# A three-layer decoder kernel: earlier neighbour similarities and their first load, first keys turned later, convolution in two bursts

## The reference

```python
na = jnp.maximum(jnp.sqrt(jnp.sum(a * a, axis=1)), EPS)
nb = jnp.maximum(jnp.sqrt(jnp.sum(b * b, axis=1)), EPS)
return jnp.sum(a * b, axis=1) / (na * nb)
```

## Time and profile before

| | |
|---|---|
| median of 3 runs | 1401.61 us (1400.67 to 1402.39) |
| profiled execution, its own time | 1403.73 us |
| its span, first to last instruction | 1401.7 us |
| PE busy | 1361.5 us (97%) |
| DVE busy | 1095.8 us (78%) |
| POOL busy | 978.7 us (70%) |
| ACT busy | 933.2 us (67%) |
| DMA queue of SP, share of 16 engines | 56.8% |

### The profile page before, as it was taken

One profiled execution on the slowest core, in us unless ns is written; L12 is line 12 of the kernel. 1 busy time (PEld: TensorE's weight loads), 2 busy tenths in 40 slices (PEclk: granted clock), 3 DMA queues, 4 the chain that ended last, 5 costly groups with the idle time before them and its releaser, 6 DMA issues.

```text
span 1401.7 us, 32338 instructions
## 1 busy us (share of the span) xinstructions
PE 1361.5 (97%) x8306; PEld 1058.0 (75%) x8306; DVE 1095.8 (78%) x3874; ACT 933.2 (67%) x3262; POOL 978.7 (70%) x932
## 2 busy tenths in 40 slices
PE   8999999999999999999997899999999999999996
PEld 5777777777777777777764688888888888888884
DVE  5887787778777777878785588777887788877877
ACT  5887888878788878878785455455554555545544
POOL 4777777767677776777775677667776677766762
PEclk9999999999999999999998999999999999999999
DMA  7344545455454545445468756676666766677652
GB/s 264 96 146 124 158 116 165 115 150 140 125 158 116 159 113 159 128 136 158 132 198 235 173 163 157 167 160 160 165 155 168 157 161 166 155 169 153 163 119 75
DMA packets 109005, 213.03 MB, mean 152 GB/s; under 512 B 26656, under 2 KB 32288, under 8 KB 108960
## 3 DMA queue, kind: packets, MB, share of 16 engines
q1 hardware_dynamic: 108624, 211.73, 56.8%
q10 hardware_dynamic: 336, 0.79, 0.2%
HBM read 131.83 MB, written 34.47 MB: 119 GB/s over the span
## 4 chain that ended last, share of the span: by engine, by line
PE 77%; SPq 6%; DMA 5%; issue 3%; DVE 3%; ACT 3%; POOL 2%; ACTq 0%; DVEq 0%; POOLq 0%
PE wo_ps L479 27%; PE wo_ps L1187 23%; PE conv_ps L1201 9%; SPq L320 4%; PE s_ps L509 4%; PE ffn_ps L1230 4%; PE pv_ps L522 3%; DMA raw<-in_xT 3%; PE ffn_ps L1249 3%; PE ffn_ps L1220 2%; ACT pexp L767 1%; PE turn_ps L498 1%; DVE sm L618 1%; DMA pt<-in_wqkv 1%; DMA att<-sim_scratch 1%
## 5 line engine op out<-in xcount | busy, mean ns | idle before, releaser
L479 PE MATMUL wo_ps<-weights,halves 128*128 128x512 f32 x2304 | 570.8, 399 | 2.8 <-DVE weights L681 2.8
L479 PEld LDWEIGHTS wo_ps<-weights,halves 128*128 128x128 f32 x2304 | 422.4, 189 | 137.7 <-issue 53.5
L767 ACT ACTIVATE pexp<-sm,smin 128x128 f32<-128x128 f32 x1024 | 398.0, 391 | 97.4 <-DVE smin L618 96.6
L1187 PE MATMUL wo_ps<-weights,halves 128*128 128x512 f32 x1464 | 395.1, 402 | 1.5 <-PEq L143 1.5
L1652 POOL TENSOR_TENSOR prods<-prod,prods 128x512 fp32r<-128x512 f32 x186 | 251.9, 1361 | 130.3 <-ACT prods L1513 125.2
L906 POOL TENSOR_TENSOR pn<-pexp,prec 128x512 f32<-128x512 f32 x256 | 265.4, 1041 | 96.2 <-DVE prec L625 96.1
L1187 PEld LDWEIGHTS wo_ps<-weights,halves 128*128 128x128 f32 x1464 | 268.1, 190 | 59.2 <-issue 2.4
L618 DVE CUSTOM_DVE_ANT_0 sm<-s_ps,mask_t 128x128 f32<-128x128 f32 x1024 | 232.0, 282 | 24.2 <-PE s_ps L509 21.8
L1513 ACT CAST prods<-prod 128x512 fp32r<-128x512 f32 x189 | 117.3, 621 | 167.0 <-DVE prod L1367 129.1
L767 ACT ACTIVATION_READ_ACCUMULATOR pexp<-sm,smin 128x1 f32 x1024 | 193.2, 189 | 0.0
L1367 DVE TENSOR_TENSOR prod<-att,x 128x512 f32<-128x512 f32 x189 | 183.0, 982 | 12.8 <-DMA att<-sim_scratch 10.1
(11 more groups left out here) (131 smaller groups left out, 1676.2 us busy)
## 6 DMA issues: line engine op xcount, KB each, us to landing
att<-sim_scratch SPq DMA_DIRECT2D x192, 252.0 KB
pt<-blocks SPq DMA_DIRECT2D x636, 64.0 KB, 2.0
ctx_t<-in_ctx SPq DMA_DIRECT2D x32, 576.0 KB, 5.2
raw<-in_xT SPq DMA_DIRECT2D x32, 512.0 KB, 4.0
xn<-in_x SPq DMA_DIRECT2D x32, 512.0 KB, 7.7
ot_scratch<-ot SPq DMA_DIRECT2D x63, 256.0 KB, 2.1
raw<-ot_scratch SPq DMA_DIRECT2D x31, 512.0 KB, 7.0
out<-late SPq DMA_DIRECT2D x31, 512.0 KB, 6.3
```

The source lines that it names most:

```text
L479: mm = pe.matmul(qkv_ps[(par + g) % 2][:], xs[:, par, xl, k], w_sb[:, wl, g, k], start=(k == 0 and n == 0), stop=(k == KT - 1 and n == 2))
L767: ins = nc.scalar.activation(pexp[:, c % 2, i * P:(i + 1) * P], sm[:, c % 2, i * P:(i + 1) * P], ACT.Exp, bias=smin[:, c % 2, i:i + 1], sc ...
L1187: mm = pe.matmul(wo_ps[n][:], os_t[:, par, ol, k], wo_sb[:, wl, k, n * BANK:(n + 1) * BANK], start=(k == 0 and m == 0), stop=(k == KT - 1 ...
```

## The change

- **Start.** PE turns the first keys ahead of slot 19 and no longer 16; POOL adds the first keys before it clears `pt`.
- **Similarities.** The sums are clamped by EPS squared before the root (in the step before the last, in place of a clamp of one column), and the clamp behind the root goes. `cosines` makes both products first and finishes `right` before `own`.
- **Stores.** ACT stores rows 0 and 1 behind its last moves of probabilities; SP stores rows 3 and 4, then row 2, and all this ahead of `store_first_half`.
- **First load.** `att` and its semaphores belong to both stages. At the end of stage one SP waits for all stores and starts the load of the first half for batch 0; stage two starts with the second half.
- **Bursts.** The six units of convolution stand ahead of slot 13 (three) and slot 4 of the next step (three), behind the expansion, which moves from slot 3 to 4. Both turns of x2 stand ahead of slot 12. The first batch keeps its own slots.
- **DVE** averages the first statistics behind `low_lt`. The buffer for dynamic DMA is set to 1024 bytes.

```diff
-    cs_edge = sem("cs_edge")
+    cs_bound = sem("cs_bound")
@@ sync, store_sims
             sp.wait_ge(sim_made, 1)
+            for n in (3, 4):
+                sp.dma_start(sim_row(sim_dram, n, 0), right).then_inc(sim_out, 16)
+            sp.wait_ge(sim_made, 2)
             sp.dma_start(sim_row(sim_dram, 2, 0), own).then_inc(own_out, 16)
-            sp.wait_ge(sim_made, 2)
-            for n, shift in ((0, 1), (1, 1), (3, 0), (4, 0)):
-                sp.dma_start(sim_row(sim_dram, n, shift), right).then_inc(sim_out, 16)
@@ sync, step of stage one
             if at_step(t, LAST):
+                store_sims()
                 store_first_half(b)
-                store_sims()
+                sp.wait_ge(own_out, 16)
+                sp.wait_ge(sim_out, 16 * 6)
+                start_att(sp, att, att_in, sim_dram, 0, 0)
@@ tensor, first batch
-                    if s == 2 * KT:
+                    if s == 2 * KT + 3:
                         pe.wait_ge(consts_in, 48)
                         turn_k(0, 0)
@@ vector
             dve.wait_ge(root, 1)
-            dve.tensor_scalar(norm, norm, COS_EPS, None, ALU.max).then_inc(cos_step, 1)
+            dve.reciprocal(norm, norm).then_inc(cos_step, 1)
+        def cosines():
             dve.wait_ge(cos_step, 1)
-            dve.reciprocal(norm, norm).then_inc(cos_step, 1)
+            dve.tensor_tensor(right, norm[:, 0:QD], norm[:, 1:QD + 1], ALU.mult).then_inc(cos_step, 1)
+            dve.tensor_tensor(own, norm[:, 0:QD], norm[:, 0:QD], ALU.mult).then_inc(cos_step, 1)
+            dve.wait_ge(cos_step, 2)
+            dve.tensor_tensor(right, right, nbs, ALU.mult).then_inc(sim_made, 1)
+            dve.wait_ge(cos_step, 3)
+            dve.tensor_tensor(own, own, sqs[:, 0:QD], ALU.mult).then_inc(sim_made, 1)
@@ vector, step B, p == 3
-                    edge = sqs[:, QD:QD + 1]
-                    dve.tensor_scalar(edge, edge, 0.0, None, ALU.max).then_inc(cs_edge, 1)
+                    dve.tensor_scalar(norm, sqs, COS_EPS * COS_EPS, None, ALU.max).then_inc(cs_bound, 1)
@@ scalar
+        def store_sims():
+            act.wait_ge(sim_made, 1)
+            for n in (0, 1):
+                act.dma_start(sim_row(sim_dram, n, 1), right).then_inc(sim_out, 16)
...
-            nc.scalar.activation(norm, sqs, ACT.Sqrt).then_inc(root, 1)
+            nc.scalar.activation(norm, norm, ACT.Sqrt).then_inc(root, 1)
...
                 if p == 7 and at_step(t, LAST):
+                    store_sims()
                     read_ot(b, 0)
@@ gpsimd
-        pool.wait_ge(w_lo, PIECES - STAGES + STAGES // 2)
-        pool.memset(pt[:], 0.0).then_inc(set_up, 1)
...
                 add_k(0, 0)
+                pool.wait_ge(w_lo, PIECES - STAGES + STAGES // 2)
+                pool.memset(pt[:], 0.0).then_inc(set_up, 1)
                 add_q(0, 0, 0)
@@ stage two
-    CONV_AT = (9, 11, 13, 15, 17, 20)
+    CONV_AT = (13, 13, 13, 20, 20, 20)
...
-        sp.wait_ge(sim_out, 16 * 6)
-        load_att(0, 0)
         load_att(0, 1)
@@ tensor, step of stage two
-                if valid(f) and s + SLOTS2 in conv_at(f):
-                    convolve(f, conv_at(f).index(s + SLOTS2))
-                if valid(c) and s in conv_at(c):
-                    convolve(c, conv_at(c).index(s))
                 if valid(z):
                     if s == 1:
                         turn_low(z)
-                    if s == 3:
+                    if s == 4:
                         expand(z)
+                for m in range(UNITS):
+                    if valid(f) and conv_at(f)[m] == s + SLOTS2:
+                        convolve(f, m)
+                    if valid(c) and conv_at(c)[m] == s:
+                        convolve(c, m)
                 if valid(f):
-                    if s in (11, 12):
-                        turn_x2(f, par, s - 11)
+                    if s == 12:
+                        turn_x2(f, par, 0)
+                        turn_x2(f, par, 1)
@@ tensor, behind the steps
+        convolve(B - 2, 3)
+        turn_low(B - 3)
         convolve(B - 2, 4)
-        turn_low(B - 3)
         convolve(B - 2, 5)
@@ vector, step of stage two
+            if valid(z):
+                low_lt(z)
+            if valid(c):
                 average(c, 0)
             if valid(z):
-                low_lt(z)
```

More of the change, by code:

```diff
@@ L124, in build @@
         kept = both.enter_context(nc.sbuf_tensor("kept", [P, D // 4 + BANK], F32))
+        att = both.enter_context(nc.sbuf_tensor("att", [P, TAPS, D], F32))
         handoff = (
@@ L139, in build @@
             both.enter_context(nc.sbuf_tensor("xn1", [P, D], F32)),
-            (kept[:, 0:D // 4], kept[:, D // 4:]))
+            (kept[:, 0:D // 4], kept[:, D // 4:]),
+            att, [both.enter_context(nc.semaphore(f"att_in{n}")) for n in range(2)])
         with ExitStack() as ctx:
@@ L165, in part1 @@
     (xn0, xn_in, o_in, o_hi, o_lo, wo_done, ot_out, ot_read, sim_made, sim_out,
-     added0, counted0, y0, stats0, xn1, kept) = handoff
+     added0, counted0, y0, stats0, xn1, kept, att, att_in) = handoff
     rope_t = sb("rope_t", [P, 2, 2, 1, DH])
@@ L728, in step @@
                 invert_norms()
-                cosine(0)
-                cosine(1)
+                cosines()
                 add_first(1)
@@ L969, in _, with start_att @@
         steps(pool, step, 0, LAST, LEAD, TAIL)
+def start_att(sp, att, att_in, sim_dram, t, h):
+    cols = slice(h * BANK, (h + 1) * BANK)
+    for (first, last), row in zip(RUNS, (0, 2, 3)):
+        sp.dma_start(att[first:last, :, cols],
+                     sim_dram[t, row, cols].unsqueeze(0).unsqueeze(0).broadcast_to([last - first, TAPS, BANK])
+                     ).then_inc(att_in[h], 16)
+    rows = sim_dram[t, 0:TAPS, cols]
+    both_edges = bass.AP(tensor=rows.tensor, offset=rows.offset, ap=[[2 * (D + SIM_PAD), 2]] + [list(d) for d in rows.ap])
+    sp.dma_start(att[EDGES[0]:EDGES[1] + 1:EDGES[1] - EDGES[0], :, cols], both_edges).then_inc(att_in[h], 16)
 def sim_row(sim_dram, n, shift):
@@ L1000, in part2 @@
     x1 = sb("x1", [P, 2, D + 2])
-    att = sb("att", [P, TAPS, D])
     prod = sb("prod", [P, PB, BANK])
@@ L1028, in part2 @@
     set_up = sem("set_up2")
-    att_in = [sem("att_in0"), sem("att_in1")]
     added = [added0] + [sem(f"added{n}") for n in range(1, 3)]
@@ L1129, in load_att @@
         def load_att(t, h):
-            cols = slice(h * BANK, (h + 1) * BANK)
             wait(sp, prod_done, after(t - 1, UNITS, TAPS * (h + 1)))
-            for (first, last), row in zip(RUNS, (0, 2, 3)):
-                sp.dma_start(att[first:last, :, cols],
-                             sim_dram[t, row, cols].unsqueeze(0).unsqueeze(0).broadcast_to([last - first, TAPS, BANK])
-                             ).then_inc(att_in[h], 16)
-            rows = sim_dram[t, 0:TAPS, cols]
-            both_edges = bass.AP(tensor=rows.tensor, offset=rows.offset, ap=[[2 * (D + SIM_PAD), 2]] + [list(d) for d in rows.ap])
-            sp.dma_start(att[EDGES[0]:EDGES[1] + 1:EDGES[1] - EDGES[0], :, cols], both_edges).then_inc(att_in[h], 16)
-        sp.wait_ge(sim_out, 16 * 6)
-        load_att(0, 0)
+            start_att(sp, att, att_in, sim_dram, t, h)
         load_att(0, 1)
```

5 lines of the change are left out of this document (2 added, 3 removed).

## The result

| | before | after |
|---|---|---|
| median (six runs each) | 1402.81 us | 1395.01 us (1392.16 to 1395.94) |
| ratio | | 0.9944 (95%: 0.9932 to 0.9957) |
| profiled execution, its own time | 1403.73 us | 1392.16 us |
| its span | 1401.7 us | 1390.1 us |

The change takes 7.8 us off the median; 7.1 were forecast, to 1394.5. On two other occasions, each beside the kernel before on one chip, the changed kernel's ratio was 0.9961 (0.9949 to 0.9973) and 0.9961 (0.9948 to 0.9973), which is 5.5 us. The three intervals overlap, so the gain is 5.5 to 7.8 us. The two profiled executions differ by 11.6 us; why that is too much is the first thing to see.

The account below looks back on a forecast made before the run. PE was taken as the bound nearly everywhere, except at the ends and handover, where it waits. Terms -1.9 - 3.0 - 1.7 - 0.5 = -7.1 us took the median from 1401.6 to 1394.5 us, range 1391.0 to 1399.0.

Parts of the forecast that it names:

- Start, -1.9: Stage one's start: PE no longer waits for the first keys, -1.9 us, between -1.0 and -2.1.
- Similarities and stores, -1.4 in the arrival: Handover: last store issued 1.9 us earlier, so att's first half reaches DVE 1.4 us earlier, bounds nothing to 1.9.
- the bound that I named: Handover: full DMA, share 1.03, means the bytes in front partly set the stores' landing; low end nothing.
- Late restart, hidden: Handover: all engines restart 2.1 us late, hidden behind PE's idle time by 1.8 us and the first normalisation by 2.5.
- the list of signs: End of prediction: handover signs were att loads near 763, restart near 764, PE idle under 3 us, clock over 0.9.
- What is late next, -3.0 for the whole handover: Handover: first convolution 1.4 us earlier, then att's second half limits if the clock holds; -3.0 us, 0 to -4.7.
- The better end of 4.2: Handover: the clock stays up over the first convolution and conv(0,5) moves from 785.98 to about 781.8.
- Bursts, -1.7: Stage two: longer runs of one matmul kind save 0.06 us a step over 29 steps, -1.7 us, 0 to -3.2.
- The half of 0.11 us: Stage two step: high end 0.11 us, 27 matmuls going from 0.2333 to 0.2293; half, 0.06, was taken.
- The margins: Stage two: time left before PE would wait: 0.9 us for the second normalisation, 0.6 us for the gates.
- Rival 4: Stage two: bursts starve PE at the turning of gated rank values in each of 29 steps; +9.1 us, 1410.7, chance 0.09.
- Tail, -0.5: Last step: last projection ends 0.7 us earlier, so DVE's addition starts earlier; -0.5 us, 0 to -0.7.

Follow-up runs that it names:

- kernel 7: The changed kernel measured again, on the chip of the PE-filled, places-in-memory and sixth-product-first kernels: 1395.86 us, ratio 0.9961.
- kernels 11: The changed kernel a third time, on another chip: 1394.83 us, ratio 0.9961.
- kernel 2: The changed kernel with convolution, turns of x2, expansion, average and tail placed as before; start and handover stay changed: 1397.0 us, ratio 0.9972.
- kernels 5: The kernel before with 20 idle matmuls on PE while it waits for the first batch's first product: 1400.69 us, ratio 0.9995.
- 6: The kernel before with only att held over both stages and the dynamic DMA scratch of 1024 bytes: 1402.31 us, ratio 1.0004.
- kernel 3: The changed kernel with the first load of att and the wait for stores back at the head of stage two: 1396.33 us, ratio 0.9965.
- kernel 10: The changed kernel with the start as before, a second time: 1396.96 us, ratio 0.9971.
- kernels 4: The changed kernel with clamp, products, stores and first load as before; start and bursts stay changed: 1395.83 us, ratio 0.9966.

## Why the prediction was right, point by point

The mechanisms came as forecast, but for the cover of the late restart (point 3). Two sizes were off, and the nearness of the first median (1395.0) to the forecast's 1394.5 is in part luck.

1. **Start, -1.9.** Right in mechanism. Where the clock did not fall, the second turn of keys is at 45.7 to 46.4 us in the old start and at 43.9 to 45.2 in the eight profiles with the new one: 1.4 us in the mean. What I missed is that the wait removed can be longer, with a fall of the clock behind it, for some 3 us more (49.8 and 48.2): 1.1 and 0.6 us of it in a later first turn of keys, 2.8 and 1.7 us between the first and the second.
2. **Similarities and stores, -1.4 in the arrival.** The last store goes out 2.1 us earlier as worked out (1.9). Of that 0.7 us is left at the load: behind the last store it took 3.7 us to the first load, and takes 5.1 now. The load goes out as the last store lands, and the DMA share from 749 to 757 us is 1.06 after, which fits the bound that I named: the bytes in front set the landing. I sat too near the upper end.
3. **Late restart, hidden.** It is later by 2.8 us in the mean, not 2.1. The step that failed in part is its cover: I gave the projections 6.6 us, but behind the longer idle time they run at the low clock for more of their length, and they last 7.9 us. In the profile after they end with the start of the first convolution: by its product it could have started near 767.9 (764.80 + 3.1, the distance in all but two rows of the table), it started at 768.33. The same happened in kernel 7 (7.92 us, 0.8 us lost); in kernels 11 and 2 they last 6.63 and 6.39 us and cost nothing. The cover was 1.8 us by my sum, and is used up in two of the three profiles of the changed kernel. In the first profile the two times themselves were right: carried to the frame of the kernel before by the last turn of keys, the first load went out at 763.19 (763.1 forecast) and the restart came at 766.05 (765.9). In the list of signs only the restart was moved to the new frame; the load, by the same 1.9 us, belongs near 761.
4. **What is late next, -3.0 for the whole handover.** It is 2.2. The clock over the first convolution stays high, as the idle time ahead of it goes, and unit 5 comes 2.1 us earlier. The better end of 4.2 was not reached, because units 3 and 5 wait for POOL and the turn of x2 waits 1.1 us for the normalisation, as foreseen.
5. **Bursts, -1.7.** Measured 1.71 in kernel 2's stretch, 0.06 a step. That longer runs are cheaper was right; the size was luck. The half of 0.11 us was picked between two ends without a reason, and the pieces of a step put 0.05 us in the projections and 0.01 in the convolutions. The margins hold: gated is ready 1.46 us behind the rank reduction (1004.84 to 1006.30) and turned at 1006.75, 0.45 us later (0.6 forecast); the second normalisation ends 4.6 us behind the burst (1012.59 to 1017.21), 0.7 us ahead of the turn (0.9). Rival 4 had 0.45 us between it and a loss in every step.
6. **Tail, -0.5.** Measured 0.62 and 0.63.

The terms as measured are 1.4 + 2.2 + 1.7 + 0.6 = 5.9 us, 1.2 under the forecast: the start was 0.5 and the handover 0.8 too large. The measured gains of 5.5, 5.5 and 7.8 us bracket both sums, so they do not tell them apart. An old start that loses its clock would add 3 us. How often that happens in the kernel before itself stays open: its one profile and those of kernels 5 and 6 show none. The two that do are kernels with the changed handover and bursts, which run long after that place.

## What to carry to other kernels

Compare two profiles by stretches between events that both have, and profile each kernel more than once before a stretch is believed: of 11.6 us between these two, 3.6 were in a stretch whose waits differ from execution to execution. Where PE is the bound and has no waits, look for the longest run of one kind of matmul that the chains behind allow; it is worth little each time (0.06 us here), but in every step, and it costs margin in those chains. A wait at a common restart belongs to all engines: before one is added, see which clock PE's next work will have, not only whether a gap covers it.

## What the runs showed of the hardware

The spacing of equal matmuls (128x512 on 128x128) depends on how long their kind has run. In the runs of 15 and 24 projections, starts are 224 to 237 ns apart for the first eight, 230 to 231 in the mean, and 226 to 227 from then on (before, after, kernels 2 and 7). Convolutions in nines stay at 227 to 238. It is no strict count: in the run of six behind the next three convolutions the spacing is down to 227 from the fourth. Between the profiles after and 7 the spacings of the same matmuls in a step differ by about 1 ns.

At the start, gaps of 2.81 and 2.95 us on PE were followed by a fall of the granted clock to its lower level; gaps of 1.36, 1.90 and 2.00 us at the same place, in the other three profiles with the old start, were not. The length of the last gap does not decide it alone: the clock stayed high over the first convolution behind 2.60 us in kernel 3, and in the tail of kernel 10 it fell behind 1.23 us, where the changed kernel kept it behind 1.24. At the restart 21 projections took 5.04 us at the high clock (kernels 4 and 6) and 6.4 to 7.9 us in the profiles with the new handover, behind gaps of 3.5 to 5.9 us.

The stores of 128 KB at the handover took 2.9 to 5.8 us to land when SP's queue had issued them and 3.2 to 4.9 us from ACT's, at a DMA share of 0.8 to 1.06 around them.
